# A scan and expert kernel on one Trainium2 core: the first scan unit ahead of the first tile, the unit loop written out, and D times the row on VectorE for the last tiles

## The reference, cut to what matters

```python
def step(h, inp):
    u_t, d_t, b_t, c_t = inp
    dA = jnp.exp(d_t[..., None] * A)
    h = dA * h + (d_t * u_t)[..., None] * b_t[:, None, :]
    y = jnp.einsum('bdn,bn->bd', h, c_t)
    return (h, y)
...
return y + D[None, :, None] * u
```

## Time and profile before

| what | value |
|---|---|
| median of 3 runs | 818.77 us (815.6 to 820.09) |
| the profiled execution's own time | 817.38 us |
| its span | 815.3 us |
| busy: VectorE, TensorE, GpSimd, ScalarE | 682.9, 663.9, 597.3, 431.0 us |
| mean granted TensorE clock | 0.913 of full speed |
| DMA moved | 118.63 MB |

### The profile page before, as it was taken

One profiled execution on the slowest core, in us unless ns is written; L12 is line 12 of the kernel. 1 busy time (PEld: TensorE's weight loads), 2 busy tenths in 40 slices (PEclk: granted clock), 3 DMA queues, 4 the chain that ended last, 5 costly groups with the idle time before them and its releaser, 6 DMA issues. The chain is left out here.

```text
span 815.3 us, 15751 instructions
## 1 busy us (share of the span) xinstructions
PE 663.9 (81%) x4538; PEld 422.7 (52%) x4539; DVE 682.9 (84%) x882; ACT 431.0 (53%) x926; POOL 597.3 (73%) x372
## 2 busy tenths in 40 slices
PE   3734889788998798989998898999889798989870
PEld 2523745245655465556655565565556555655550
DVE  5769777579999999999999999999999999997110
ACT  1324656465655556656655575566557554653320
POOL 3728800038788898988989898888989898889532
PEclk9866955599999989999999998999999998999995
DMA  7972659979944754674575466547645654662322
GB/s 228 371 259 91 180 206 297 321 221 241 210 102 103 144 118 87 146 150 94 115 163 111 89 149 138 105 90 164 139 90 125 134 127 90 142 142 35 49 27 26
DMA packets 76845, 118.63 MB, mean 146 GB/s; under 512 B 22456, under 2 KB 56848, under 8 KB 74512
## 3 DMA queue, kind: packets, MB, share of 16 engines
q1 hardware_dynamic: 54656, 90.95, 41.2%
q0 software_dynamic: 19824, 27.16, 19.4%
q10 hardware_dynamic: 2336, 0.15, 0.2%
HBM read 82.87 MB, written 35.27 MB: 145 GB/s over the span
## 5 line engine op out<-in xcount | busy, mean ns | idle before, releaser
L534 POOL TENSOR_TENSOR ring<-ring,bc 128x1024 f32<-128x1024 f32 (+2 forms) x128 | 308.0, 2424 | 38.9 <-DVE state L1047 38.0
L1044 DVE TENSOR_TENSOR_SCAN ring<-ring,state,pb 128x512 f32<-128x512 f32 x256 | 313.8, 1267 | 4.6
L654 ACT ACTIVATE ring<-late,aneg 128x512 f32<-128x512 f32 x256 | 164.2, 721 | 12.0 <-DMA late<-dd_d 9.1
L1035 DVE TENSOR_TENSOR pb<-fb,bc 128x1024 f32<-128x1024 f32 x128 | 157.3, 1229 | 3.0
L1284 PE MATMUL py<-w2x,pool 128*128 x568 | 141.6, 395 | 0.5 <-ACT pool L726 0.3
L1267 PE MATMUL fa<-w,pool 128*128 x284 | 137.7, 608 | 3.9 <-issue 2.8
L506 POOL DMA_INDIRECT out_dram<-pool,meta x71 | 112.9, 1590 | 29.8 <-issue 15.7
L1267 PE MATMUL fb<-w,pool 128*128 x284 | 134.3, 596 | 0.0
L486 POOL DMA_INDIRECT pool<-xn_d,meta x71 | 71.3, 1004 | 81.3 <-DVE ids L1001 33.5
L1284 PEld LDWEIGHTS py<-w2x,pool 128*128 128x128 f32 x568 | 107.7, 200 | 13.6 <-issue 1.0
L1267 PEld LDWEIGHTS fb<-w,pool 128*128 128x128 f32 x284 | 54.5, 192 | 68.9 <-issue 68.9
(11 more groups left out here) (213 smaller groups left out, 752.8 us busy)
## 6 DMA issues: line engine op xcount, KB each, us to landing
late<-dd_d SPq DMA_DIRECT2D x256, 128.0 KB
bc<-bc_d SPq DMA_DIRECT2D x72, 256.0 KB
w<-in_L_ffn_w_dram SPq DMA_DIRECT2D x16, 512.0 KB, 8.6
ring<-in_L_attn_x_dram SPq DMA_DIRECT2D x8, 512.0 KB, 4.3
out_dram<-ring SPq DMA_DIRECT2D x8, 512.0 KB, 7.7
xn_d<-w2x SPq DMA_DIRECT2D x8, 512.0 KB, 8.6
dd_d<-pool SPq DMA_DIRECT2D x8, 512.0 KB
dd_d<-ring SPq DMA_DIRECT2D x8, 512.0 KB, 5.1
```

The source lines that it names most:

```text
L534: ins = po.tensor_tensor(r, r, c_rows, ALU.mult)
L654: ins = ac.activation(ring[:, g % RING, n, :], dd[:, g % 2, 0, :], ACT.Exp, scale=aneg[:, NH * g + n:NH * g + n + 1])
L1035: ve.tensor_tensor(pb[:, :].rearrange("p (n c) -> p n c", n=2), pd[:, :].rearrange("p (o c) -> p o c", o=1).to_broadcast([P, 2, CH]), b_ro ...
L1044: ve.tensor_tensor_scan(r, r, pb[:, CH * m:CH * m + CH], state[:, NH * g + n:NH * g + n + 1], ALU.mult, ALU.add).then_inc(S["scan_done"], 1)
```

## The change

- **Order.** ScalarE runs exps and put_du of unit 0 first; for unit 0 it waits only for its dd loads and for the end of VectorE's preparation (`pr_du`), and the waits for the stores move to the first place that overwrites their source (units 1 and 2, tiles 0 and 2). VectorE runs unit 0, then before each further unit u the SiLU of tile u - 1. So tiles 63 to 70 lie behind the last unit, and the stores of tiles 61 to 70.
- **Loops.** All 64 units are written out on all engines; indices are constants.
- **Adds.** Tile j is added in unit j + 2. ye has three buffers, ya two (no hand_over, no yb, no idb). The last chunk's four scan adds come behind tile 65 and wait for it alone, not for each other.
- **Meta.** It is loaded for 8 tiles at once into two halves. At the fourth unit of chunk c (c from 1 on), ahead of load_dd of the next unit, SP waits until tile 8c - 1 is added. Six gather buffers in place of four.
- **Last unit.** VectorE does the second half of its multiply by the C rows.
- **Tiles from 63 on.** No D matmuls: VectorE multiplies the gathered row by weight and by D (128 x 256, loaded once into drow), and makes the output from PSUM, weight and this row; ScalarE's evac_y goes there.
- **SP at the start.** It issues the weight loads of experts 2 and 3 ahead of load_dd(2).

```diff
-SPI = G
-SCAN_STEPS = (3, 3, 7, 7)
-REST = range(SPI * NCH + 1, FT)
+UNITS = NCH * G
+REST = UNITS - 1
+SCAN_UNITS = {3: (0, 1), 7: (2, 3)}
+XR, XT, YE = 6, 4, 3
+BLOCK = G
...
+        def landed_expert(j):
+
+            return 16 * (1 + j + 1 + scans_by(unit_of_expert(j)) + (TPC if j > LAST_SCANS else 0))
...
+            for u in range(UNITS):
+                c, g = u // G, u % G
+                if u == UNITS // 2:
+                    sp.dma_start(drow, ds_in.rearrange("(o d) -> o d", o=1).to_broadcast([P, D])).then_inc(S["drow_in"], 16)
+                if u >= 2:
+                    load_dd(u)
+                if c == 0 and g + EARLY < E:
+                    load_up(g + EARLY, w3, w3_in)
+                    load_down(g + EARLY)
+                if g == 3 and c + 1 < NCH:
+                    if c:
+                        sp.wait_ge(S["hc_done"], G * c)
+                    sp.wait_ge(S["bc_in"], 128 * (c + 1))
+                if 3 <= g < 3 + P // DG and c + 1 < NCH:
+                    load_bc(c + 1, g - 3)
+                if g == 3 and c:
+                    sp.wait_ge(S["meta_in"], 16 * (c + 1))
+                    sp.wait_ge(S["added"], landed_expert(BLOCK * c - 1))
+                    load_meta(c + 1)
...
+            for u in range(UNITS):
+                c, g = u // G, u % G
+                j = u - 2
+                if j >= 0:
+                    gather(j + XR)
+                scans = SCAN_UNITS.get(g, ()) if c else ()
+                split = 1 if scans else NH // 2
+                po.wait_ge(S["h_ready"], u + 1)
+                done = multiply(u, slice(0, split))
+                for n in scans:
+                    add_scan(c - 1, n, landed_scan(c - 1, scans[0]) - 16)
+                if u < UNITS - 1:
+                    done = multiply(u, slice(split, NH))
+                elif split < NH // 2:
+                    done = multiply(u, slice(split, NH // 2))
+                done.then_inc(S["hc_done"], 1)
+                if j >= 0:
+                    add_expert(j)
+            for j in range(UNITS - 2, FT):
+                if j + XR < FT:
+                    gather(j + XR)
+                add_expert(j)
+                if j == LAST_SCANS:
+                    for n in range(TPC):
+                        add_scan(NCH - 1, n, landed_expert(j))
...
+                if u == 0:
+                    ac.wait_ge(S["pr_du"], KC * NCH)
+                elif u == 1:
+                    ac.wait_ge(S["bc_put1"], 32 * NCH // 2)
+                    ac.wait_ge(S["dd_put10"], 16 * NCH // 2)
+                elif u == 2:
+                    ac.wait_ge(S["dd_put11"], 16 * NCH // 2)
...
+            exps(0)
+            put_du(0)
+            evac_xt(0)
+            exps(1)
+            for u in range(1, FT + 1):
+                j = u - 1
+                tanh(j)
+                if u < UNITS:
+                    put_du(u)
+                if j:
                     evac_ht(j - 1)
+                if 3 <= u < UNITS + 3:
+                    take_y(u - 3)
+                if 2 <= u < UNITS + 2:
+                    take_sum(u - 2)
                 if j + 1 < FT:
+                    evac_xt(j + 1)
+                if u + 1 < UNITS:
+                    exps(u + 1)
+                if j and j <= REST:
+                    evac_y(j - 1)
...
+            for u in range(UNITS):
+                if u:
+                    silu(u - 1)
+                half_unit(u, 0)
+                half_unit(u, 1)
+                keep_states(u)
...
+            def skip_row(j):
+
+                ve.wait_ge(S["xtr_done"], j + 1)
+                x = xr[j % XR]
+                ve.scalar_tensor_tensor(x, x, meta[:, j % (2 * BLOCK), 1:2], drow, ALU.mult, ALU.mult).then_inc(S["rest_row"], 1)
+
+            def take_out(j):
+
+                ve.wait_ge(S["w2_done"], j + 1)
+                ve.wait_ge(S["rest_row"], j - REST + 1)
+                ve.wait_ge(S["ye_done"], j + 1)
+                ve.wait_ge(S["added"], landed_expert(j - YE))
+                ve.scalar_tensor_tensor(ye[j % YE], py[:, 0:D], meta[:, j % (2 * BLOCK), 1:2], xr[j % XR], ALU.mult,
+                                        ALU.add).then_inc(S["ye_done"], 1)
+
+            ve.wait_ge(S["drow_in"], 16)
+            for j in range(REST, FT):
+                skip_row(j)
+                silu(j)
+                if j > REST:
+                    take_out(j - 1)
+            take_out(FT - 1)
```

More of the change, by code:

```diff
@@ L243, in apart, with experts_by, scans_by, unit_of_expert @@
             eng.sem_inc(S["passed"], 1)
[L245 to L265, removed]
+        def experts_by(u):
+            return max(0, u - 1)
+        LAST_SCANS = UNITS + 1
+        def scans_by(u):
+            c, g = u // G, u % G
+            return 0 if c == 0 else (c - 1) * TPC + sum(len(SCAN_UNITS[k]) for k in SCAN_UNITS if k <= g)
+        def unit_of_expert(j):
+            return min(j + 2, UNITS - 1)
+        def landed_expert(j):
+            return 16 * (1 + j + 1 + scans_by(unit_of_expert(j)) + (TPC if j > LAST_SCANS else 0))
+        def landed_scan(c, n):
+            u = (c + 1) * G + next(k for k in SCAN_UNITS if n in SCAN_UNITS[k])
+            return 16 * (1 + experts_by(u - 1) + c * TPC + n + 1)
         @block.sync
@@ L491, in _ @@
             po.wait_ge(S["pr_ids"], NCH - 1)
[L492 to L493 removed]
+            gather(0)
+            gather(1)
             for h in range(KC):
                 po.wait_ge(S[f"dd_put0{h}"], 16 * NCH // 2)
[L496 to L507 removed]
@@ L509, in add_scan @@
-            def add_scan(turn, c, n, beside=0):
-                po.wait_ge(S["yb_done"], c + 1)
-                if not isinstance(c, int):
-                    apart(po)
-                po.wait_ge(S["added"], landed(turn - 1 - beside))
-                apart(po)
-                po.indirect_dma_start(out[:, :], bass.IndirectOffsetOnAxis(ap=idb[:, n:n + 1], axis=0), yb[:, n, :], None,
-                                      compute_op=ALU.add).then_inc(S["added"], 16)
-            po.wait_ge(S["acc_put"], 16 * NCH)
@@ L541, in _ @@
-            turn(0)
-            with po.Fori(1, NCH) as c:
-                turn(c)
-            for i, (kind, n) in enumerate(REST_ADDS):
-                if kind == "expert":
-                    if n + 4 < FT:
-                        gather(n + 4, (n + 4) % SPI)
-                    add_expert(REST_TURN + i, n, n % SPI, n % 2)
-                else:
-                    add_scan(REST_TURN + i, NCH - 1, n)
-            po.wait_ge(S["added"], landed(REST_TURN + len(REST_ADDS) - 1))
+            for j in range(2, XR):
+                gather(j)
```

486 lines of the change are left out of this document (170 added, 316 removed).

## The result

The changed kernel takes 834.74 us (median of 4 runs, 831.35 to 838.95), the kernel before on the same chip 818.21 (815.6 to 820.09). The ratio is 1.0207, 95% interval 1.0151 to 1.0262: 2.1% slower. The prediction, 814.5 with a range up to 820.0, was wrong, and on the other side. The profiled execution took 834.0 us, its span is 832.2.

What follows compares the result with a forecast made beforehand. VectorE's pace over 64 units, then GpSimd's chain of stores, was taken as the bound. Last scan 4.8 us earlier, tail 0.5 later: net -4.3, from 817.38 to 813.1 profiled, 814.5 as median; range 804.5 to 820.

Steps and rivals of the forecast that it cites:

- Head: Start of the kernel: unit 0 ahead of tile 0 brings the first product 8.6 us sooner, unit 2's 6.2 us.
- Loop written out: Units 2 to 63: every pitch 8.89 us, so 6.4 us of loop costs go.
- Tail: Behind the last scan: two tiles more but fewer steps in a row in GpSimd's chain of stores, 0.5 us longer.
- The wait added on SP: Ahead of units 8c+4, c = 2 to 7: VectorE stalls 1.3 us six times, 7.8 us, bounds 0 and 18.
- old waits: VectorE's existing waits between the scans, for the w3 matmul and ScalarE's tanh: 2.1 us, left in.
- VectorE's pace hides them: Gather ring, buffer and meta load edits on ScalarE, GpSimd and SP during the scans: priced at nothing.
- B: Scan stretch: late output copy delays TensorE's next w1 matmul, 12 us added, +7.7 us net, 826.5; chance 0.10.
- A: Scan stretch: SP's added wait is hidden, no stall; -12.1 us, 806.7; chance 0.25.
- C: Tail: bound by its tiles if the granted clock falls, 4 us late at the end, 818.8; chance 0.10.
- D: Scan stretch: written-out code still runs at the loop's cost, 6.4 us more, 820.9; chance 0.05.

Runs made afterwards that it cites:

- e4: The kernel before with only its loops written out on all engines; 815.10 us, ratio 0.9922.
- e11: e1 with the tail's D matmuls and output copy back on TensorE and ScalarE, as in the kernel before; 801.33 us, ratio 0.9898 to the kernel before.
- e1: The changed kernel with three meta blocks, so SP's wait asks for a tile eight earlier; 810.68 us, ratio 0.9892 to the kernel before.
- e2: The changed kernel with SP's meta wait and load two units later, at unit 8c+5; 805.72 us, ratio 0.9810 to the kernel before.
- e6: The changed kernel with three meta blocks and SP's wait asking for one tile sooner, 8c-2; 800.23 us, ratio 0.9872 to the kernel before.
- e8: e1 with load_dd(2) issued ahead of the weights of experts 2 and 3; 798.58 us, ratio 0.9862 to the kernel before.
- e14: e6 with load_dd(2) issued ahead of the weights of experts 2 and 3; 803.39 us, ratio 0.9920 to the kernel before.
- e13: e6 with a chunk's eight bc loads issued at once behind the dd loads of unit 8c+5; 835.57 us, ratio 1.0294 to the kernel before.
- e7: The changed kernel with all bc loads of the next chunk issued ahead of SP's wait; 818.80 us, ratio 1.0115 to the kernel before.
- e12: The changed kernel with bc loads and unit 8c+4's dd loads both ahead of SP's wait; 814.87 us, ratio 1.0044 to the kernel before.
- e9: The changed kernel with unit 8c+4's dd loads ahead of SP's wait, bc loads behind; 820.55 us, ratio 1.0117 to the kernel before.

## Why the prediction was wrong

The prediction for the profiled execution was 813.1, measured were 834.0. The 20.9 us, step by step:

- **Head: right in kind, 2.3 us short.** First product 162.2 predicted, 163.69 measured; unit 2's product 182.4 and 184.66. load_dd(2) ended ScalarE's wait at 180.26, just past my upper bound of 180; the 177.8 took one MB more as 3.2 us. The 174.5 that I worked out from the fit in the Trainium skill, "DMA: Bandwidth & Descriptors", section on the anatomy of one DMA, is further off. The fit is given per DMA and for GpSimd's path; this load went over SP's queue behind 2 MB of weights.
- **Loop written out: right.** 6.4 us predicted; pitches of 8.89 over chunk ends, and e4 gains 6.4 us (4.3 to 8.5).
- **Tail: right.** The last add starts at T + 60.5 (T + 60.1 predicted); e11 confirms that the tiles do not bind. From it to the end are 0.5 us more than before, so the tail is 0.9 us longer than predicted.
- **The wait added on SP: the step that failed.** I wrote a stall of 1.3 us at six units, 7.8 us, with bounds of 0 and 18. The stalls at 8c+4 are 11.1 us, six times 1.3 to 2.4: the mechanism with its place stands, 3.3 us too small. But I ended the account there, with "it has the next unit with scan adds, where it waits for GpSimd anyway, to catch up", it being TensorE. With the 2.1 us of old waits my excess was 9.9; measured are 27.9. The other 14.8 us stand at 8c+2 and elsewhere. The runs in which the wait is met in time (e1, e2, e6, e8, e11, e14) have an excess of 1.8 to 6.8, so the wait costs 21 to 26 us, above my upper bound of 18. All but a few us of the 14.8 come by a path I did not follow.
- **That path.** I priced what stands behind the wait only for the engine that needs the first load. I did not ask what all of it does when it is let go at once: it fills the DMA engines just when GpSimd issues the tile add that its scan pair waits for. GpSimd comes late, the fold on TensorE waits for it, and VectorE stalls two to three units on. e13 shows this part alone: the loads bunched, no late wait, 2.9% lost. e7 shows it from the other side: bc out of the burst, nothing at 8c+2.
- **GpSimd's slack.** I had put the edits on GpSimd at nothing ("VectorE's pace hides them"), though the trace of before shows adds, gather and multiply filling 499.8 of 576.3 us in the earlier trace rows, and the scan pairs on top of an even load. 1.5 us per chunk do not hide a wait of 3 to 9 us.

Of the prediction's rivals, B had the sign (826.5, chance 0.10; 834.74 measured) and a stall passed on along ScalarE and TensorE; but it began with TensorE's w1 matmul behind a late output copy, while the chain seen begins with GpSimd. A is refuted by the stalls at 8c+4, C by e11, D by e4. The range was too narrow because it was built from the forecast and A, with B left outside.

Not settled: how the 14.8 us divide between the burst's delay of the adds and the clock. After TensorE has waited for GpSimd, the granted clock from 434 to 444 us is 0.83 of full speed, part of the time at 1.2 GHz in place of 2.4; from 424 to 434 it is 1.00. The clock may well have a large part in it. Ahead of the stall at unit 26 it is 0.79 (395 to 403 us), ahead of the one at unit 28 it is 1.00 (416 to 424). In unit 27 of e12 the fold waited 2.75 us for GpSimd, the clock stayed at 1.00 (428 to 436 us), and no stall followed; in the same unit of e9 the fold waited 6.37, the clock was 0.75 (428 to 438 us), and 3.7 us were lost. No run separates the two. And e12 leaves open whether the wait at its place, for this tile, costs nothing once neither load nor burst is behind it; no run here had that.

## What to carry to other kernels

A wait added to an in-order DMA queue has two prices: the first load behind it comes late, and all loads behind it come at once. Price both, and look for the engine with the least slack that waits for a small transfer in that moment, here GpSimd's chain of accumulating stores. If a buffer's reuse needs such a wait, put it where it is already met (asking for one tile sooner was worth 3% here, waiting two units later 4%) and keep the loads spread.

## What the runs showed of the hardware that was not expected

- **A small accumulating store lands very late beside plain loads.** One tile's 128 rows: under 5.2 us where the next add need not wait (e6), 4.56 per step alone in the tail, 7.8 in the changed kernel's burst, 8.5 in e9, 13.5 in e13 with 2 MB of loads in front. The Trainium skill, "DMA: Bandwidth & Descriptors", section on queues, rings and completion order, has each DMA engine take turns, packet by packet, between the queues that have work. By that rule alone my estimate is a doubling at most, from 4.56 to 9.1 us; 13.5 is beyond it. The same page, in its section on back-pressure in remote DMA, says that a saturated destination port stalls an engine's other queues as well; these transfers are not remote. The trace shows a part of it in e13: the add is issued at 412.43, but its queue (q0) has no packet from 413 to 419 us, while SP's queue (q1) fills all engines; from 419 to 424 both have packets. First the window 413 to 419, then 419 to 424 (packets, MB, share of 16 engines):

```profile
q1 hardware_dynamic: 238, 1.30, 103.7%
...
q1 hardware_dynamic: 258, 0.85, 68.9%
q0 software_dynamic: 188, 0.25, 27.6%
```

In the changed kernel's burst q0 has none from 420.3 to 424 either; in e6 and in the tail of the kernel before its packets begin about 2.1 us behind the issue. So at least 4.4 of e13's 9 us are lost before the first packet, which is not a taking of turns. What holds the packets back, no run here tells.

- **Full DMA engines at less than full rate.** In the bursts the share is 1.00 to 1.06 at 218 to 225 GB/s; in the earlier trace rows 1.09 went with 331 GB/s. The dd and bc loads write 32 partitions each, the weights all 128; whether that is the cause was not tried.
- **A turn of the hardware loops costs about 0.9 us.** In the earlier trace rows a pitch is 0.64 us longer over a turn's end and 0.04 at the seven others. Writing out the loops of the kernel before, on all engines, gave 6.4 us over 7 turns. Which engine's loop it was, was not tried apart.
